# Sparse experts of a two-layer graph network: full-width weight loads in the up product and full-height ones in the down product

## The chip, the cores and the metric

The kernel is one program on one core of one Trainium2 chip. The metric is the device time of one execution in microseconds (us), from runs on the chip; lower is better. Everything is float32 in the part that is changed.

## The reference, cut to what matters

The model has two layers, each a graph attention, a linear attention and a mixture of experts, over 3,125 nodes with 256 features. The last step of the second layer is the one that is changed: each node goes to the one expert of 32 that its router scores highest, through 64 hidden features and back to 256:

```python
idx = jnp.argmax(xf @ router_w.T + router_b, axis=-1)         # 32 experts
h = relu(einsum('nd,ndh->nh', xf, W1[idx]) + b1[idx])         # 256 -> 64
out = relu(einsum('nh,nhd->nd', h, W2[idx]) + b2[idx])        # 64 -> 256
```

## The kernel before, in words

The program is a row of stages, each with its own block of engine programs; all engines meet between two stages. The stage here is `experts_l1` (L2651), between the router (`finish_route_l1`) and `combine_l1`. The router has sorted the nodes by expert into 56 tiles of 128 rows (`slots1` in device memory), each tile with one expert, whose number stands in `K.expert_at`. `combine_l1` gathers the results back to the nodes (L2816, 25 indirect transfers on POOL), adds the layer's input (L2823) and writes the output.

`experts_l1` handles tile j in slot q = j mod 4 of its buffers:

- SP loads the expert's weights `w[:, q, :]` (L2678): per partition 2 x 64 columns of the up matrix (two halves of 64 columns, one for each half of the 256 input features), then 256 columns of the down matrix. The down matrix has 64 weight rows, row 64 is its bias, and rows 65 to 127 are zeros that the host puts there.
- ACT loads the tile's rows (L2731), two tiles ahead in its own program. Both loads of a slot wait for the down product of the tile that used the slot four tiles before (`s_y`).
- PE turns the rows over (`turn_rows`, L2687, two transposes against the identity), multiplies by the up weights (`up`, L2695, two float32 products; each is recorded as two weight loads and two matmuls) and by the down weights (`down`, L2702, one product, likewise two and two). Its order is fixed: `turn_rows(j+1)`, `up(j)`, `down(j-1)`, again and again. `turn_rows` waits for both loads of its tile.
- DVE copies the turned rows out of PSUM (L2760) and takes the relu of the result (L2767); ACT takes the relu of the hidden features with the up bias (L2748) into `h_t[0:64]`. Row 64 of `h_t` is set to one at the stage's start (L2782), for the down bias.
- POOL stores the result (L2799), and waits at the end for all stores.

The stationary operand of `up` is the up weights: 128 rows by 64 columns, with 128 moving columns of turned features. The stationary operand of `down` is `h_t[0:65]`: 65 rows by 128 columns, with 256 moving columns of down weights.

Of the kernel before, what the change touches and what calls it, by code (L numbers as in the profile page):

```python
# [26 lines left out]
P = 128  # L27
N = 3125
D = 256
# [21 lines left out]
E1, F1 = 32, 64  # L51
# [2599 lines left out]
def experts_l1(prog, K, A):  # L2651

    with Stage(prog, "moe1") as st:
        Q, U2 = 4, 2
        sizes = {"rows": D, "w": 2 * F1 + D, "xs_t": 2 * P, "h_t": P, "y": D}
        at, tile = 0, {}
        for name, n in sizes.items():
            tile[name] = K.arena_a[:, at:at + Q * n].rearrange("p (q n) -> p q n", q=Q)
            at += Q * n
        rows, w, xs_t, h_t, y = tile.values()  # L2660
        w1, w2 = w[:, :, 0:2 * F1], w[:, :, 2 * F1:]
        b1 = st.sbuf("b1", [F1, E1])
        ps_t, ps_h, ps_y = (st.psum(n, [P, U2, 512]) for n in ("ps_t", "ps_h", "ps_y"))
        s_in = [st.sem(f"in{q}") for q in range(Q)]
        s_out = [st.sem_sw(f"out{q}") for q in range(Q)]
        s_b, s_one, s_t, s_xt, s_h, s_ht, s_y, s_yb = (st.sem(n) for n in ("b", "one", "t", "xt", "h", "ht", "y", "yb"))
        turns = T1 // Q
        block = st.block()

        @block.sync  # L2670
        def _(sp):
            sp.dma_start(b1[:, :], A["f1_b1"]).then_inc(s_b, 16)
            with sp.Fori(0, turns) as i:
                for q in range(Q):
                    j = i * Q + q
                    expert = sp.value_load(K.expert_at[0:1, bass.ds(j, 1)], min_val=0, max_val=E1 - 1)
                    sp.wait_ge(s_y, j + 1)
                    sp.dma_start(w[:, q, :], A["f1_w"][expert]).then_inc(s_in[q], 16)  # L2678

        @block.tensor  # L2680
        def _(pe):
            def turn_rows(i, q):
                j = i * Q + q
                pe.wait_ge(s_in[q], 32 * (i + 1))
                pe.wait_ge(s_xt, j + 1)
                for k in range(2):
                    ins = pe.transpose(ps_t[:, q % U2, k * P:(k + 1) * P], rows[:, q, k * P:(k + 1) * P], K.ident[:, :])  # L2687
                ins.then_inc(s_t, 1)

            def up(i, q):  # L2690
                j = i * Q + q
                pe.wait_ge(s_xt, j + 1 + U2)
                pe.wait_ge(s_ht, j + 1)
                for k in range(2):
                    ins = pe.matmul(ps_h[0:F1, q % U2, 0:P], lhsT=w1[:, q, k * F1:(k + 1) * F1], rhs=xs_t[:, q, k * P:(k + 1) * P], start=(k == 0), stop=(k == 1))  # L2695
                ins.then_inc(s_h, 1)

            def down(i, q):
                j = i * Q + q
                pe.wait_ge(s_ht, j + 1 + U2)  # L2700
                pe.wait_ge(s_yb, j + 1)
                pe.matmul(ps_y[:, q % U2, 0:D], lhsT=h_t[0:F1 + 1, q, :], rhs=w2[0:F1 + 1, q, :], start=True, stop=True).then_inc(s_y, 1)  # L2702

            def turn(i, head=False, tail=False):
                for q in range(Q):
                    if q + 1 < Q:
                        turn_rows(i, q + 1)
                    elif not tail:
                        turn_rows(i + 1, 0)
                    up(i, q)  # L2710
                    if q:
                        down(i, q - 1)
                    elif not head:
                        down(i - 1, Q - 1)

            pe.sem_inc(s_h, Q)
            pe.sem_inc(s_y, Q)
            pe.wait_ge(s_one, 1)
            turn_rows(0, 0)
            turn(0, head=True)  # L2720
            with pe.Fori(0, turns - 2) as i:
                turn(i + 1)
            turn(turns - 1, tail=True)
            down(turns - 1, Q - 1)

        @block.scalar
        def _(act):
            def load(i, q):
                j = i * Q + q
                act.wait_ge(s_y, j + 1)  # L2730
                act.dma_start(rows[:, q, :], K.slots1[bass.ds(j * P, P), :]).then_inc(s_in[q], 16)  # L2731

            act.sem_inc(s_ht, U2)
            load(0, 0)
            load(0, 1)
            act.wait_ge(s_b, 16)

            def turn(i, tail=False):
                for q in range(Q):
                    j = i * Q + q  # L2740
                    if q + 2 < Q:
                        load(i, q + 2)
                    elif not tail:
                        load(i + 1, q + 2 - Q)
                    expert = act.value_load(K.expert_at[0:1, bass.ds(j, 1)], min_val=0, max_val=E1 - 1)
                    act.wait_ge(s_h, j + 1 + Q)
                    act.wait_ge(s_y, j + 1)
                    act.activation(h_t[0:F1, q, :], ps_h[0:F1, q % U2, 0:P], ACT.Relu, bias=b1[:, bass.ds(expert, 1)]).then_inc(s_ht, 1)  # L2748

            with act.Fori(0, turns - 1) as i:  # L2750
                turn(i)
            turn(turns - 1, tail=True)

        @block.vector
        def _(dve):
            def turned(i, q):
                j = i * Q + q
                dve.wait_ge(s_t, j + 1)
                dve.wait_ge(s_h, j + 1)
                dve.tensor_copy(xs_t[:, q, :], ps_t[:, q % U2, 0:2 * P]).then_inc(s_xt, 1)  # L2760

            def result(i, q, stored=True):
                j = i * Q + q
                dve.wait_ge(s_y, j + 1 + Q)
                if stored:
                    dve.wait_ge(s_out[q], 16 * i)
                dve.tensor_scalar(y[:, q, :], ps_y[:, q % U2, 0:D], 0.0, None, ALU.max).then_inc(s_yb, 1)  # L2767

            def turn(i, tail=False):
                for q in range(Q):  # L2770
                    if q + 1 < Q:
                        turned(i, q + 1)
                    elif not tail:
                        turned(i + 1, 0)
                    if isinstance(i, int) and i * Q + q == 0:
                        continue
                    back = (i, q - 1) if q else (i - 1, Q - 1)
                    result(*back, stored=not (isinstance(i, int) and back[0] == 0))

            dve.sem_inc(s_xt, U2)  # L2780
            dve.sem_inc(s_yb, U2)
            dve.memset(h_t[F1:F1 + 1, :, :], 1.0).then_inc(s_one, 1)  # L2782
            turned(0, 0)
            turn(0)
            turn(1)
            with dve.Fori(0, turns - 3) as i:
                turn(i + 2)
            turn(turns - 1, tail=True)
            result(turns - 1, Q - 1)

        @block.gpsimd
        def _(pool):
            st.clear_stale(pool)
            with pool.Fori(0, turns) as i:
                for q in range(Q):
                    j = i * Q + q
                    pool.wait_ge(s_yb, j + 1 + U2)
                    pool.nop(nofuse=True)
                    pool.dma_start(K.y_slots1[bass.ds(j * P, P), :], y[:, q, :]).then_inc(s_out[q], 16)  # L2799
            for q in range(Q):  # L2800
                pool.wait_ge(s_out[q], 16 * turns)
# [33 lines left out]
def stages(prog, K, A, out):  # L2835

    order_edges(prog, K, A)
    items_project_l0(prog, K, A)
    linear_attention_l0(prog, K, A)
    edge_scores_l0(prog, K, A)  # L2840
    segment_softmax(prog, K, "soft0", H0, C0, A=A)
    aggregate_l0(prog, K)
    finish_route_l0(prog, K, A)
    experts_l0(prog, K, A)
    join_project_l1(prog, K, A)
    linear_attention_l1(prog, K, A)
    for H, C, RW, table, kept, acc in ((H1, C1, H1 * (DH1 + 1), K.table1, K.kept1, K.acc1),
                                       (1, C2, D + 1, K.table2, K.kept2, K.acc2)):
        keep = K.al[:, WSP * H:WSP * (2 * H + 1)].rearrange("p (s h) -> p s h", h=H + 1)
        edge_scores_l1(prog, K, f"score_h{H}", H, C, RW, table, kept, A)  # L2850
        segment_softmax(prog, K, f"soft_h{H}", H, C, keep, RW, table, kept)
        aggregate(prog, K, f"sum_h{H}", H, RW, table, kept, acc, keep)
        if H == H1:
            middle_l1(prog, K, A)
    finish_route_l1(prog, K, A)
    experts_l1(prog, K, A)
    combine_l1(prog, K, out)
# [119 lines left out]
```

## Time and profile before

| | us |
|---|---|
| median of 3 runs (lowest, highest) | 3234.79 (3234.34 to 3239.66) |
| span of the profiled execution | 3241.8 |
| mean granted TensorE clock over the span | 0.801 |
| stage `experts_l1`, first turned tile to last down product | 3019.6 to 3190.0 |

The profiled execution's span is 7.0 us (0.2%) above the median of the runs; no other time is recorded for it. Its clock column gives the share of the full TensorE clock that was granted: 1.00 is 2.4 GHz, 0.50 is 1.2 GHz. PE is the matmul half of TensorE and PEld the weight loads. A DMA row ending in q is an issue, which isn't counted as busy time. The ends of matmuls are modelled, the starts are recorded.

### The profile page before, as it was taken

Reading aid. Unit: us, or ns where it says so; the run is one execution under the profiler, and the core shown is the slowest. Engines: PE = TensorE matmul, PEld = TensorE weight load, DVE = VectorE, ACT = ScalarE, POOL = GpSimd, SP = SyncE. Lnnn points to the kernel's source line nnn. Section 1 sums busy time; section 2 is a strip of 40 time slices with the busy share of each in tenths; the row PEclk is TensorE's granted clock in tenths of the full one; section 3 lists DMA queues with packets and bytes.
Section 4 is the critical chain, followed back from the end, with each engine's and each line's share of the span. In section 5 each row is a group of like instructions: output and inputs, shape, how many; then the busy total and the mean of one; then the engine's idle time right before and its main releaser. Section 6 shows DMA issues by size and latency. Waiting matters only on the chain. (4 is left out here: it accounts for less than half of the span.)

```text
span 3241.8 us, 48906 instructions
## 1 busy us (share of the span) xinstructions
PE 2228.9 (69%) x10992; PEld 1503.4 (46%) x10993; DVE 2056.2 (63%) x3849; ACT 1246.0 (38%) x3616; POOL 1722.4 (53%) x1802
## 2 busy tenths in 40 slices
PE   3635777767997389948673899997661766654693
PEld 2322333335555356535562677776551444433341
DVE  7587777778788343452677788887682666665221
ACT  2223333326775221234001666665201666652010
POOL 1586777733554301132554777774466777751213
PEclk9867787778999599979766999998765899885555
DMA  4768888874885278825996788886896555530454
GB/s 140 205 181 231 260 263 262 261 235 138 218 219 161 96 254 278 263 90 197 364 396 196 243 274 269 273 276 166 240 291 175 148 147 149 146 107 23 132 152 132
DMA packets 456713, 668.49 MB, mean 206 GB/s; under 512 B 67154, under 2 KB 334092, under 8 KB 456001
## 3 DMA queue, kind: packets, MB, share of 16 engines
q1 hardware_dynamic: 334017, 357.96, 36.3%
q0 software_dynamic: 87248, 261.86, 27.3%
q10 hardware_dynamic: 35296, 46.90, 4.1%
q8 instruction: 64, 1.05, 0.1%
q14 instruction: 88, 0.72, 0.1%
HBM read 491.69 MB, written 176.23 MB: 206 GB/s over the span
## 5 line engine op out<-in xcount | busy, mean ns | idle before, releaser
L1533 POOL DMA_INDIRECT xn<-table,src_col x572 | 595.8, 1042 | 180.6 <-issue 148.9
L1574 PE MATMUL sum_h_ps<-xn,sum_h_hot 128*128 128x261 f32 (+1 forms) x1936 | 526.5, 415 | 192.0 <-DVE xn L1588 128.8
L1574 PEld LDWEIGHTS sum_h_ps<-xn,sum_h_hot 128*128 128x128 f32 x1936 | 369.7, 201 | 341.3 <-DVE xn L1588 251.6
L1092 POOL DMA_INDIRECT arena_a<-table,src_col x264 | 265.6, 1006 | 267.7 <-issue 184.7
L978 POOL DMA_INDIRECT arena_b<-table,src_col x336 | 318.7, 949 | 111.7 <-issue 108.6
L1588 DVE TENSOR_TENSOR xn<-xn,al 128x514 f32<-128x514 f32 (+1 forms) x352 | 243.4, 692 | 167.9 <-DMA xn<-table,src_col 164.0
L1597 DVE TENSOR_TENSOR arena_a<-arena_a,sum_h_ps 128x522 f32 (+1 forms) x440 | 246.1, 559 | 62.1 <-issue 38.2
L1707 PE MATMUL sum_ps<-xn,sum_hot 128*128 128x264 f32 x880 | 245.4, 406 | 31.4 <-DVE arena_a L1730 10.4
L1690 POOL TENSOR_TENSOR xn<-xn,al 128x264 f32<-128x264 f32 x220 | 158.8, 723 | 168.5 <-DMA xn<-edge_h 165.5
L1009 ACT ACTIVATE xn<-score_ps_en 128x512 f32<-128x512 f32 x220 | 131.4, 597 | 291.1 <-PE score_ps_en L995 287.4
L999 PE MATMUL score_ps_hd<-arena_a,score_hot 128*128 x1320 | 238.8, 330 | 0.0
L1707 PEld LDWEIGHTS sum_ps<-xn,sum_hot 128*128 128x128 f32 x880 | 151.9, 191 | 124.6 <-issue 88.1
L995 PE MATMUL score_ps_en<-enc_rows,score_attr 30*128 30x256 bf16 x440 | 101.2, 317 | 130.8 <-DVE xn L1037 85.7
L1040 DVE TENSOR_REDUCE al<-xn 128x528 f32 (+1 forms) x220 | 154.7, 703 | 32.8 <-DVE xn L1037 32.0
L999 PEld LDWEIGHTS score_ps_hd<-arena_a,score_hot 128*128 128x128 bf16 x1320 | 129.1, 112 | 91.4 <-issue 61.3
L756 POOL DMA_INDIRECT xn<-table,src_col x104 | 124.9, 1201 | 84.8 <-issue 84.8
L1574 PE MATMUL sum_h_ps<-arena_b,sum_h_hot 128*128 128x261 f32 x704 | 166.8, 383 | 0.9 <-DVE arena_b L1588 0.6
L1559 ACT ACTIVATE xn<-xn,al 128x129 f32<-128x129 f32 x528 | 167.2, 388 | 0.0
L1555 ACT ACTIVATE xn<-al 128x4 f32<-128x4 f32 (+1 forms) x352 | 71.2, 203 | 238.3 <-DMA xn<-table,src_col 237.4
L1037 DVE TENSOR_TENSOR xn<-xn,score_ps_hd 128x528 f32<-128x528 f32 x220 | 153.4, 697 | 14.2 <-PE score_ps_hd L999 13.2
L1540 ACT ACTIVATE sum_h_away<-iota_row,rel_col 128x128 f32<-128x128 f32 x440 | 149.2, 386 | 11.1 <-DVE sum_h_one L1600 11.1
L2053 POOL DMA_DIRECT2D y_slots<-al x32 | 28.4, 888 | 220.0 <-DVE al L2029 219.9
(516 smaller groups left out, 4628.7 us busy)
## 6 DMA issues: line engine op xcount, KB each, us to landing
xn<-edge_h SPq DMA_DIRECT2D x220, 264.0 KB, 3.2
edge_h<-arena_b SPq DMA_DIRECT2D x84, 528.0 KB
arena_b<-kept SPq DMA_DIRECT2D x66, 516.0 KB, 5.4
xn_t<-edge_rows SPq DMA_DIRECT2D x110, 256.0 KB, 4.6
score_h_hot<-hots SPq DMA_DIRECT2D x220, 128.0 KB, 11.7
kept<-arena_a ACTq DMA_DIRECT2D x40, 516.0 KB, 9.1
xn<-kept SPq DMA_DIRECT2D x66, 257.0 KB
arena_a<-in_f_w SPq DMA_DIRECT2D x16, 1024.0 KB, 8.7
```

The lines of the kernel that those rows point to most:

```text
L978: pool.indirect_dma_start(rows[:, q, k, :], None, K.table0[:, :], bass.IndirectOffsetOnAxis(ap=K.src_col[:, g * GS + k:g * GS + k + 1], ax ...
L999: ins = pe.matmul(ps_hd[:, m, s, 0:D + H], lhsT=hot[:, q, edges[s]], rhs=near[:, window, c, :], start=(c == 0), stop=(c == 2))
L1037: dve.tensor_tensor(prod[:, m, :].rearrange("p (s d) -> p s d", s=SUB), enc[:, m, :].rearrange("p (s d) -> p s d", s=SUB), ps_hd[:, m, :, ...
L1040: dve.tensor_reduce(al[:, bass.ds(w * SUB, SUB), :], prod[:, m, :].rearrange("p (s h r) -> p s h r", s=SUB, h=H), AX, ALU.add).then_inc(s_ ...
L1092: pool.indirect_dma_start(rows[:, q, s, :], None, table, bass.IndirectOffsetOnAxis(ap=K.src_col[:, w * SUB + s:w * SUB + s + 1], axis=0)). ...
L1533: pool.indirect_dma_start(rows[w][:, s, 0:RW], None, table, bass.IndirectOffsetOnAxis(ap=K.src_col[:, w * SUB + s:w * SUB + s + 1], axis=0 ...
L1559: ins = act.activation(cols, cols, ACT.Copy, scale=al[:, w * SUB + 1, h:h + 1])
L1574: ins = pe.matmul(ps[:, u, b, 0:part], lhsT=hot[:, w % QH, s, :], rhs=rows[w][:, s, b * part:(b + 1) * part], start=(s == 0), stop=(s == S ...
L1588: dve.tensor_tensor(view, view, al[:, bass.ds(w * SUB, HALF), :].rearrange("p s h -> p (s h)").unsqueeze(2).broadcast_to([P, HALF * H, RW ...
L1597: dve.tensor_tensor(out, out, ps[:, j % U2, :, 0:part], ALU.add).then_inc(s_acc, 1)
L1690: pool.tensor_tensor(view, view, al[:, bass.ds(w * SUB + 1, 1), :].rearrange("p s h -> p (s h)").unsqueeze(2).broadcast_to([P, H, R]), ALU ...
L1707: ins = pe.matmul(ps[:, u, 0:ROW0], lhsT=hot[:, q, s, :], rhs=rows[:, q, s, :], start=(s == 0), stop=(s == SUB - 1))
```

## The change

`up` loads 128 columns in place of 64. The first of its two products takes columns 0 to 127 of the slot (both halves of the up matrix), the second columns 64 to 191 (the second half and 64 columns of the down matrix). It writes 128 partitions of PSUM, of which ACT reads the first 64 as before. `down` uses all 128 rows of `h_t` and of the down weights, whose rows 65 to 127 are zeros; so that those rows of `h_t` hold numbers, they are set to zero at the start of the stage, ahead of row 64.

```diff
-        w1, w2 = w[:, :, 0:2 * F1], w[:, :, 2 * F1:]
+        w2 = w[:, :, 2 * F1:]
...
-                    ins = pe.matmul(ps_h[0:F1, q % U2, 0:P], lhsT=w1[:, q, k * F1:(k + 1) * F1], rhs=xs_t[:, q, k * P:(k + 1) * P], start=(k == 0), stop=(k == 1))
+                    ins = pe.matmul(ps_h[:, q % U2, 0:P], lhsT=w[:, q, k * F1:k * F1 + P], rhs=xs_t[:, q, k * P:(k + 1) * P], start=(k == 0), stop=(k == 1))
...
-                pe.matmul(ps_y[:, q % U2, 0:D], lhsT=h_t[0:F1 + 1, q, :], rhs=w2[0:F1 + 1, q, :], start=True, stop=True).then_inc(s_y, 1)
+                pe.matmul(ps_y[:, q % U2, 0:D], lhsT=h_t[:, q, :], rhs=w2[:, q, :], start=True, stop=True).then_inc(s_y, 1)
...
+            dve.memset(h_t[F1:, :, :], 0.0).then_inc(s_zero, 1)
+            dve.wait_ge(s_zero, 1)
             dve.memset(h_t[F1:F1 + 1, :, :], 1.0).then_inc(s_one, 1)
```

## Rows read from the trace of the kernel before

**Rows 1.** The page: the granted clock in 40 slices of the span, in tenths.

```profile
PEclk9867787778999599979766999998765899885555
```

**Rows 2.** The chain that ended last, by line.

```profile
by line: POOL xn L2816 0.7%; issue 0.2%; DMA xn<-y_slots,slot_to 0.1%; DVE xn L2823 0.0%; POOLq L121 0.0%; PEldq L121 0.0%
```

**Rows 3.** Stretches: length, each engine's busy us (instructions), granted clock, DMA share, GB/s.

```profile
280.00:700.00 420.00, 312.83 (x1734) 151.39 (x1731) 330.95 (x557) 139.50 (x301) 310.08 (x327) 0.79 0.88 259
1140.00:1380.00 240.00, 220.35 (x773) 140.32 (x774) 95.47 (x139) 49.86 (x72) 26.80 (x29) 0.98 0.81 263
2500.00:2880.00 380.00, 260.85 (x840) 164.62 (x840) 232.52 (x419) 263.12 (x850) 289.81 (x297) 0.90 0.55 148
2915.00:2955.00 40.00, 31.59 (x148) 28.94 (x146) 27.80 (x96) 20.53 (x52) 0.00 (x0) 0.50 0.00 0
3020.00:3190.00 170.00, 158.42 (x448) 84.30 (x446) 46.87 (x111) 20.28 (x56) 29.20 (x54) 0.50 0.48 146
```

**Rows 4.** One such stretch of the first layer's edge scores.

```profile
425.00:435.00 10.00, 9.44 (x39) 4.28 (x40) 8.58 (x14) 3.22 (x7) 7.56 (x9) 0.50 0.82 256
```

**Rows 5.** Timeline of PE inside it.

```profile
427.53 0.60 PE L995 MATMUL score_ps_en<-enc_rows,score_attr 30*128 30x256 bf16 x2
428.06 1.50 PE L999 MATMUL score_ps_hd<-arena_a,score_hot 128*128 x6
```

**Rows 6.** Groups of the stage by form: rows*columns of the weights, shape, count, mean ns.

```profile
L2695 PEld LDWEIGHTS moe_ps_h<-arena_a 128*64 128x64 f32 x224 | 40.1, 218 | 18.8 <-issue 18.8
...
L2687 PEld LDWEIGHTS moe_ps_t<-ident,arena_a 128*128 128x128 f32 x112 | 16.2, 204 | 102.1 <-issue 75.5 <-DMA arena_a<-slots 23.2 <-DMA arena_a<-in_f_w 3.3
```

**Rows 7.** Timeline of the stage: start us, length us, what.

```profile
3024.41 1.22 PE L2702 MATMUL moe_ps_y<-arena_a 65*128 65x256 f32 x2
...
3105.20 0.68 PE L2687 MATMUL moe_ps_t<-ident,arena_a 128*128 128x128 f32 x2
...
3105.49 0.36 ACTq L2731 DMA_DIRECT2D arena_a<-slots  x1
3105.81 1.12 PE L2695 MATMUL moe_ps_h<-arena_a 128*64 128x128 f32 x4
...
3106.86 1.22 PE L2702 MATMUL moe_ps_y<-arena_a 65*128 65x256 f32 x2
...
3108.26 0.37 ACTq L2731 DMA_DIRECT2D arena_a<-slots  x1
...
3108.36 0.69 PE L2687 MATMUL moe_ps_t<-ident,arena_a 128*128 128x128 f32 x2 [0.28 <-DMA arena_a<-slots]
...
3111.35 0.69 PE L2687 MATMUL moe_ps_t<-ident,arena_a 128*128 128x128 f32 x2
...
3187.89 2.08 PE L2702 MATMUL moe_ps_y<-arena_a 65*128 65x256 f32 x4
```

**Rows 8.** DMA issues of the stage: count, KB each, median us to landing.

```profile
arena_a<-in_f_w SPq DMA_DIRECT2D x54, 192.0 KB, 2.7
...
arena_a<-slots ACTq DMA_DIRECT2D x53, 128.0 KB, 2.9
```

**Rows 9.** Timeline: runs of like float32 matmuls in other stages, at either clock.

```profile
179.79 6.38 PE L774 MATMUL mix_ps_c<-arena_a 128*128 128x128 f32 x52
204.70 4.64 PE L774 MATMUL mix_ps_c<-arena_a 128*128 128x128 f32 x20 [18.54 <-DVE arena_a L850]
...
1165.06 7.17 PE L2002 MATMUL moe_ps_y<-arena_a,arena_b 128*128 128x256 f32 x32 [0.62 <-DVE al L2029]
```

**Rows 10.** The stretch that holds the second of those runs.

```profile
200.00:220.00 20.00, 4.64 (x20) 4.34 (x20) 18.36 (x16) 2.67 (x2) 16.34 (x13) 0.50 0.60 172
```

**Rows 11.** Groups of weight loads over the whole span: the longest mean.

```profile
L1835 PEld LDWEIGHTS route_ps_l<-route_gw,xn_t 128*128 128x128 f32 x100 | 24.1, 333 | 1.0 <-ACT xn_t L1861 1.0
```

**Rows 12.** Timeline of the stage's start.

```profile
3015.61 0.48 DVE L2782 MEMSET arena_a<- 1x512 f32 x1 [33.32 <-PEq L2716]
...
3019.63 0.66 PE L2687 MATMUL moe_ps_t<-ident,arena_a 128*128 128x128 f32 x2 [53.74 <-DMA arena_a<-in_f_w]
```

More of the change, by code:

```diff
@@ L2665, in experts_l1 @@
         s_out = [st.sem_sw(f"out{q}") for q in range(Q)]
-        s_b, s_one, s_t, s_xt, s_h, s_ht, s_y, s_yb = (st.sem(n) for n in ("b", "one", "t", "xt", "h", "ht", "y", "yb"))
+        s_b, s_zero, s_one, s_t, s_xt, s_h, s_ht, s_y, s_yb = (st.sem(n) for n in ("b", "zero", "one", "t", "xt", "h", "ht", "y", "yb"))
         turns = T1 // Q
```

## The prediction

> **What bounds the kernel now.** I read the page first. Its clock line [rows 1] ends in four slices at 5: the last 320 us run at half of TensorE's clock, and `experts_l1` lies in them. The chain that ended last [rows 2] names only the closing gathers of `combine_l1`. These begin when all engines have met behind `experts_l1`, so a microsecond taken from that stage is one taken from the kernel, as long as the stores behind the last tile keep their length.
>
> Then the stretches [rows 3]. In the stage PE is busy 158.42 of 170 us (93%), with a granted clock of 0.50 (1.2 GHz) from end to end. No long stretch with full weights looks so: 1140 to 1380, the first layer's experts, has PE at 92% and 0.98; 2500 to 2880 has PE at only 69% and still 0.90. What differs is the size of the weights. In the stage they are 128 rows by 64 columns and 65 rows by 128 columns, beside transposes of 128 by 128 [rows 6, 7]; in the experts of the first layer they are nearly all 128 by 128. The stretch from 280 to 700 lies between: its loop has two matmuls over 30 rows for each six over 128 [rows 5], PE is busy 74%, and the clock 0.79. For 425 to 435 us PE was busy 94% there and the clock stayed at 0.50 [rows 4]. So in this trace a TensorE that is busy by the record, with part of its rows unused, is held at 1.2 GHz, and one with full weights isn't. The trace can't say whether rows or columns do it; the change fills both.
>
> That PE is 93% busy doesn't make it the only bound. The timeline [rows 7] shows the loop of one tile as turn, up, down. The down products start at 3024.41 and, for the last two, from 3187.89 on; 54 steps lie between, so a tile takes 163.48 / 54 = 3.03 us. PE's own work of one turn is shorter: turn to up 3105.20 to 3105.81 (0.61), up to down 1.05, down's 1.22 with 0.1 of it overlapped by what follows, about 2.8. The rest is waiting for the row load: a turn starts at 3108.36 on "DMA arena_a<-slots". The load of tile j+3 is issued when `down(j-1)` has ended, and is wanted two turns on. So two tiles take (start of a turn to the issue) + (issue to the start of the turn that wants it): 3105.20 to 3108.26 is 3.06; 3105.49 to 3108.36 is 2.87 and 3108.26 to 3111.35 is 3.09, mean 2.98. Together 6.04, half of it 3.02, which is the measured 3.03. The landings agree: 2.9 and 2.7 us in the median for rows and weights [rows 8]. What PE gains comes out at half its size per tile, since it shortens only the first part of that two-tile loop.
>
> **The change part by part.** *Arithmetic and DMA.* No instruction, wait or transfer is added in the loop; the host's zeros were loaded already. The counts stay as they are.
>
> *Streaming.* The moving columns stay at 128 and 256, so at an equal clock the matmuls take what they took.
>
> *Weight loads of up, 64 to 128 columns.* This is the part that could cost. In L774, also float32 with 128 moving columns but 128 weight columns, 20 matmuls took 4.64 us at 0.50 [rows 9, 10]: (4.64 - 0.42 for the last one's length) / 19 = 0.222 us each. The loads lie hidden beside the matmuls. Up's four take 1.05 us to the start of down with the change to another wait in it, so they run at that step already. In this stage the transposes' 128-column loads take 204 ns against 218 for up's 64 columns [rows 6]. I take 0. Bound above: the longest mean of a 128x128 float32 load in the trace, 333 ns [rows 11], less 218 is 0.115 each, 0.46 per up group, if fully exposed.
>
> *Rule against the change.* The rows show 204 ns for 128 columns and 218 for 64. The Trainium skill, "TensorE: Matmul & The Clock Gate", section "LDWEIGHTS (loading the stationary operand)", says that a load takes its number of columns divided by 1.2 ns whatever its rows; by that up's loads would grow by an estimated 53 ns a pass, and the down loads not at all. The trace disagrees for the durations as recorded. By this rule, with all exposed, the loop would be slower by an estimated 0.1 us a tile.
>
> *Down over 128 rows.* Rows are parallel; 0. Nothing below 0 is excluded for its loads, but they have no measured share of the loop.
>
> *Memset.* One more of 64 partitions by 512, beside the one of 1 by 512 that took 0.48 us, and a wait [rows 12]. Call it 0.5 to 1.0. It ends by 3017.1 where PE's first turn waits for the weights' DMA until 3019.63. Hidden, with 2.5 us to spare; uncovered it would cost at most 1 us.
>
> *The clock.* With full weights I expect the 0.50 to end. The worth of 1.00 from pairs of rows [rows 9]: L774 at 1.00 takes (6.38 - 0.28) / 51 = 0.120 us per 128 moving columns, against 0.222; L2002 at 1.00 takes (7.17 - 0.38) / 31 = 0.219 for 256. So each 128 columns saves 0.102. From the start of a turn to the issue lie two of 128 (turn), four of 128 (up), two of 256 (down): ten units, 1.02 us; the last matmul's tail shortens too (0.42 to 0.28, the two subtracted lengths, of which the streaming step explains 0.10), so 1.02 to 1.15, say 1.1. Two tiles then take 6.04 - 1.1 = 4.94, a tile 2.47 in place of 3.02: 0.55 us less. PE's own turn is then about 2.8 - 1.1 = 1.7, so the DMA loop still binds, now alone. Over 54 steps at full clock for all: 30 us.
>
> *How much of the stage gets it.* At 1.00 PE would be busy some 1.7 to 1.75 of 2.47 us, 70%; the stretch from 2500 to 2880, full weights at 69% busy, has 0.90. Then it isn't sure how soon the half-clock loop with its waits wakes the clock; 280 to 700 comes to 0.79. And here, a faster PE only waits longer for its row loads in each turn, after which a fall is likelier. Between 0.50 and 1.00 I take a mean of 0.75: half of 30 us, 15 us. DMA isn't in the way: its share is 0.48 [rows 3] and would rise to 0.48 x 3.02 / 2.75 = 0.53, and POOL's stores are a third of the bytes.
>
> **The sum.** 0 + 0 + 0 (memset hidden) - 15 = -15 us. Against the profiled execution: 3241.8 - 15 = 3226.8. That execution is 7.0 us above the median of the runs and no row says why; the same difference from the median gives 3234.8 - 15 = 3220.
>
> **The rivals.** *A, my forecast:* the clock goes up and down in the stage, mean 0.6 to 0.93; 54 x 0.55 x (0.2 to 0.86) = 6 to 26 us: 3209 to 3229.
>
> *B, full clock nearly throughout.* For it: 0.98 to 1.00 in the other stages with full weights. Against it: those don't wait 0.7 us in every tile for a DMA. 26 to 32 us off: 3203 to 3209.
>
> *C, the change doesn't do what it can: the clock stays at 0.50.* For it: the router's short matmuls from 2915 to 2955 have full weights too, PE 79% busy, and 0.50 [rows 3]; and the stage waits on its loads already. Then 0, and 3234 to 3236. The Trainium skill, same page, "Part 1: The HAM clock gate", says that the clock gate is opened by how busy PE has been and says nothing of the weights' size; by that rule 93% busy would have had full clock before, and filling the weights would change nothing. The trace disagrees on the first half with its 0.50.
>
> *D, the other side: up's weight loads become the step.* Place: between the four matmuls of `up`. They decide once a 128-column load takes longer than the 0.222 us of the matmul beside it. Price: up to 0.46 a group, in the two-tile loop 0.23 a tile, 54 x 0.23 = 12 us, 3247, with the clock unchanged. Against it: L774's 20 matmuls at 0.222 with such loads [rows 9].
>
> **How the numbers follow.** A 0.58, B 0.13, C 0.24, D 0.03, and 0.02 for anything else that is slower. 0.2% of the time, 6.5 us, is about what a measurement of this kernel can tell from no change. A gives faster but for its lower edge (0.02 of it within), B faster: 0.69. C with A's edge gives the same: 0.26. D and the rest give slower: 0.05. The likeliest is A's middle, 3220. The range reaches from B, 3203, to C's end, 3236, and leaves out D.
>
> **What would show each step.** The granted clock over 3020 to 3190 in the new profile: A says 0.6 to 0.93, with whole stretches of ten us at 1.00, C 0.50. Step of `down` to `down`: 2.4 to 2.5 us where the clock is 1.00, still 3.0 where it is 0.50 (D: 3.2). The recorded loads of up: near 200 ns at 0.50. Turns that wait on "DMA arena_a<-slots" or "in_f_w" in nearly every tile, and issue to landing still 2.7 to 3.0. The first turn still released by a DMA, not by L2782's memset. All before the stage unchanged. The prediction fails on its size if the clock's mean is far from 0.75, and in its mechanism if the clock rises and the step of a tile doesn't fall by half of PE's saving, or if landings grow as the loads come closer together.

## The result and the profile after

The changed kernel takes 3197.29 us in the median (3192.84 to 3198.91, 4 runs), the kernel before 3234.57 (3228.68 to 3239.66, 4 runs). The ratio is 0.9877, with a 95% interval of 0.9861 to 0.9893: 37 us or 1.2% faster. That is below the low end of the range, 3203, and more than twice the 15 us of the forecast.

The whole stage after, as one stretch (length, busy us and instructions of PE, PEld, DVE, ACT and POOL, granted clock, DMA share, GB/s):

```profile
3013.00:3145.70 132.70, 84.22 (x448) 60.85 (x448) 46.86 (x111) 20.28 (x56) 29.22 (x54) 0.91 0.62 186
```

The same stretch of before, from the first turn to the last down product, has 170.4 us at 0.50; [rows 3] show nearly the same. So 37.7 us went in the stage, which is the gain of the medians. The profiled spans differ by 44.5 (3241.8 to 3197.3), and the first turn starts at 3013.07 in place of 3019.63: that 6.6 us lies ahead of the changed code. In the kernels run below, whose code is the same up to there, the first turn starts anywhere from 3012.7 to 3028.4, so it is scatter.

The clock isn't at 1.00 throughout. Ten-microsecond stretches of the stage after:

```profile
3010.00:3020.00 10.00, 5.17 (x20) 4.08 (x21) 1.88 (x6) 0.72 (x2) 0.59 (x1) 0.50 0.51 142
3020.00:3030.00 10.00, 7.03 (x35) 4.91 (x34) 3.34 (x9) 1.45 (x4) 2.11 (x4) 0.80 0.62 184
...
3040.00:3050.00 10.00, 6.21 (x39) 4.20 (x37) 3.99 (x10) 1.81 (x5) 2.18 (x5) 1.00 0.66 205
...
3090.00:3100.00 10.00, 6.35 (x31) 4.81 (x31) 3.08 (x8) 1.45 (x4) 2.06 (x5) 0.83 0.60 183
```

The groups by form, to be held against [rows 6]:

```profile
L2695 PEld LDWEIGHTS moe_ps_h<-arena_a 128*128 128x128 f32 x224 | 34.6, 221 | 0.2
...
L2687 PE MATMUL moe_ps_t<-ident,arena_a 128*128 128x128 f32 x112 | 26.9, 325 | 102.1 <-DMA arena_a<-in_f_w 56.4 <-DMA arena_a<-slots 45.7
...
L2702 PEld LDWEIGHTS moe_ps_y<-arena_a 128*128 128x128 f32 x112 | 19.5, 218 | 0.6 <-ACT arena_a L2748 0.6
```

The number behind the last bar is the loader's idle time, and it is the surprise. Before, the weight loader stood idle for 18.8 us ahead of up's loads, put down to "issue" [rows 6]; now it is 0.2. Ahead of down's loads 18.4 us before (first line below) have become 0.6. The turns wait 45.7 us for the row loads: the two-tile loop binds. The kernel before, a whole-stage group and two lines of its timeline:

```profile
L2702 PEld LDWEIGHTS moe_ps_y<-arena_a 65*128 65x128 f32 x112 | 28.3, 313 | 18.4 <-issue 18.2
```

```profile
3105.81 0.72 PEld L2695 LDWEIGHTS moe_ps_h<-arena_a 128*64 128x64 f32 x4 [0.33 <-issue]
...
3106.86 0.50 PEld L2702 LDWEIGHTS moe_ps_y<-arena_a 65*128 65x128 f32 x2 [0.33 <-issue]
```

The timeline after, first at 0.50 and then at 1.00, to be held against [rows 7]:

```profile
3019.17 0.69 PE L2687 MATMUL moe_ps_t<-ident,arena_a 128*128 128x128 f32 x2 [1.02 <-DMA arena_a<-slots]
...
3021.45 0.69 PE L2687 MATMUL moe_ps_t<-ident,arena_a 128*128 128x128 f32 x2
...
3021.72 0.97 PEld L2695 LDWEIGHTS moe_ps_h<-arena_a 128*128 128x128 f32 x4
3021.74 0.38 ACTq L2731 DMA_DIRECT2D arena_a<-slots  x1
3021.93 1.06 PE L2695 MATMUL moe_ps_h<-arena_a 128*128 128x128 f32 x4
...
3022.78 1.06 PE L2702 MATMUL moe_ps_y<-arena_a 128*128 128x256 f32 x2
...
3112.75 0.37 ACTq L2731 DMA_DIRECT2D arena_a<-slots  x1
3113.26 0.44 PE L2687 MATMUL moe_ps_t<-ident,arena_a 128*128 128x128 f32 x2 [0.69 <-DMA arena_a<-slots]
...
3113.53 0.61 PE L2695 MATMUL moe_ps_h<-arena_a 128*128 128x128 f32 x4
...
3113.98 0.60 PE L2702 MATMUL moe_ps_y<-arena_a 128*128 128x256 f32 x2
...
3114.75 0.38 ACTq L2731 DMA_DIRECT2D arena_a<-slots  x1
3115.61 0.20 PEld L2687 LDWEIGHTS moe_ps_t<-ident,arena_a 128*128 128x128 f32 x2 [1.44 <-DMA arena_a<-slots]
...
3117.89 0.43 PE L2687 MATMUL moe_ps_t<-ident,arena_a 128*128 128x128 f32 x2 [0.96 <-DMA arena_a<-slots]
```

At 0.50 up to down is 3022.78 - 3021.93 = 0.85 us, where it was 1.05 at the same clock [rows 7], and start of a turn to the issue of a load is 3019.17 to 3021.74 = 2.57 in place of 3.06. Up's first load begins at 3021.72, 0.21 ahead of its matmul at 3021.93; before, load and matmul both began at 3105.81. So the change took time away at an equal clock too, which the prediction didn't have. At 1.00 start of a turn to issue is 3113.26 to 3114.75 = 1.49, and issue to the turn that wants it 2.86 and 3.14 (3112.75 to 3115.61, 3114.75 to 3117.89): (1.49 + 3.0) / 2 = 2.25 us a tile. Over the stage the down products start 2.35 us apart, counted as in the prediction: (3144.22 - 3017.09) / 54. The rest is the part at 0.50.

### The profile page after: what moved, and what is told of

The parts are those of the page before. It is cut to its first block and busy times, and to the rows that moved or that the text cites. A ratio compares the mean times of both kernels' runs of the same rounds, so it can differ in the third digit from the quotient of the medians.

```text
span 3197.3 us, 48907 instructions
## 1 busy us (share of the span) xinstructions
PE 2147.4 (67%) x10992; PEld 1473.6 (46%) x10993; DVE 2060.7 (64%) x3850; ACT 1246.2 (39%) x3616; POOL 1712.0 (54%) x1802
## 3 DMA queue, kind: packets, MB, share of 16 engines
q8 instruction: 64, 1.05, 0.1%
## 5 line engine op out<-in xcount | busy, mean ns | idle before, releaser
L1533 POOL DMA_INDIRECT xn<-table,src_col x572 | 587.4, 1027 | 180.6 <-issue 150.1
L756 POOL DMA_INDIRECT xn<-table,src_col x104 | 124.3, 1195 | 85.4 <-issue 84.7
```

The source lines that it names most:

```text
L1533: pool.indirect_dma_start(rows[w][:, s, 0:RW], None, table, bass.IndirectOffsetOnAxis(ap=K.src_col[:, w * SUB + s:w * SUB + s + 1], axis=0 ...
```

## The experiments

Two theories stood: all of the gain is the clock; or PE lost time at up's and down's odd shapes, at either clock, and the clock is only a part. Each experiment was timed against the kernel before.

### 1. Up alone

```diff
# against before
-                    ins = pe.matmul(ps_h[0:F1, q % U2, 0:P], lhsT=w1[:, q, k * F1:(k + 1) * F1], rhs=xs_t[:, q, k * P:(k + 1) * P], start=(k == 0), stop=(k == 1))
+                    ins = pe.matmul(ps_h[:, q % U2, 0:P], lhsT=w[:, q, k * F1:k * F1 + P], rhs=xs_t[:, q, k * P:(k + 1) * P], start=(k == 0), stop=(k == 1))
```

> Up loads 128 columns; down keeps its 65 rows, no extra memset. Clock theory (all of the gain is the granted clock): if columns open it, about 0.9 in the stage and some 30 us off; if rows or the whole area do, 0.50 and 0 us. Shape theory (PE loses time wherever neighbouring weights differ in shape, at either clock): turn to up falls from 0.61 to 0.43 us and up's first step from 0.268 to 0.213, up to down stays near 0.35 after the last matmul of up, and the two-tile loop gives back 0.1 us a tile, 5 us in all, at 0.50.

Measured: 3219.44 us, ratio 0.9952 (0.9935 to 0.9969), 15.5 us off. The stage, and its groups by form:

```profile
3012.60:3164.30 151.70, 126.55 (x448) 89.90 (x448) 47.15 (x112) 20.28 (x56) 29.20 (x54) 0.55 0.53 163
```

```profile
L2695 PEld LDWEIGHTS moe_ps_h<-arena_a 128*128 128x128 f32 x224 | 52.4, 321 | 0.1
```

The clock hardly moves (0.55), and the loader's idle time is gone with up alone. The timeline has start of a turn to issue 2.57 us and up to down 0.86:

```profile
3100.82 0.69 PE L2687 MATMUL moe_ps_t<-ident,arena_a 128*128 128x128 f32 x2 [0.51 <-DMA arena_a<-slots]
...
3101.30 1.06 PE L2695 MATMUL moe_ps_h<-arena_a 128*128 128x128 f32 x4
...
3102.16 1.06 PE L2702 MATMUL moe_ps_y<-arena_a 65*128 65x256 f32 x2
...
3103.39 0.37 ACTq L2731 DMA_DIRECT2D arena_a<-slots  x1
```

The gain is three times the 5 us that the shape theory asked for. The late start inside down goes too (its two matmuls take 1.06 us in place of 1.22), though down still has 65 rows. So it was never down's rows that cost time there; it was that up's narrow weights stood before it. The loop gives 0.49 / 2 = 0.25 us a tile, 54 x 0.25 = 13 us. The rest, 2 to 3 us, is what a clock of 0.55 is worth: full clock for a tenth of the stage, 0.1 x 0.55 x 54 = 3 us by the prediction's price.

### 2. Down alone

```diff
# against before, with the memset of the change
-                pe.matmul(ps_y[:, q % U2, 0:D], lhsT=h_t[0:F1 + 1, q, :], rhs=w2[0:F1 + 1, q, :], start=True, stop=True).then_inc(s_y, 1)
+                pe.matmul(ps_y[:, q % U2, 0:D], lhsT=h_t[:, q, :], rhs=w2[:, q, :], start=True, stop=True).then_inc(s_y, 1)
```

> Down uses 128 rows, with the memset; up keeps its 64 columns. Clock theory by rows: the clock is near 0.9 and 25 to 30 us are off; by area or columns: 0.50 and 0 us. Shape theory: the step between down's two matmuls falls from 0.588 to 0.427 us, turn to up stays 0.61 (at 0.50), 0.08 us a tile less, 4 us in all without the clock.

Measured: 3211.69 us, ratio 0.9928 (0.9904 to 0.9951), 23 us off.

```profile
3014.60:3158.50 143.90, 106.86 (x448) 59.64 (x448) 46.76 (x111) 20.30 (x56) 29.35 (x54) 0.87 0.56 172
```

```profile
L2695 PEld LDWEIGHTS moe_ps_h<-arena_a 128*64 128x64 f32 x224 | 27.3, 157 | 12.2 <-issue 12.2
L2702 PEld LDWEIGHTS moe_ps_y<-arena_a 128*128 128x128 f32 x112 | 18.9, 212 | 11.5 <-issue 11.2 <-ACT arena_a L2748 0.3
```

Filling the rows brings the clock to 0.87; the loader's idle time stays. At 1.00 up to down is 3106.73 - 3106.15 = 0.58 us here, where the changed kernel has 0.45, and down's pair takes 0.70 against 0.60:

```profile
3101.32 1.22 PE L2702 MATMUL moe_ps_y<-arena_a 128*128 128x256 f32 x2
...
3106.15 0.65 PE L2695 MATMUL moe_ps_h<-arena_a 128*64 128x128 f32 x4
3106.73 0.70 PE L2702 MATMUL moe_ps_y<-arena_a 128*128 128x256 f32 x2
```

The forecast of the shape theory for this run, a shorter step inside down, missed: at 0.50 down's pair still takes 1.22 us (at 3101.32), as before the change. The drops of the ratio of the two halves, 0.0048 and 0.0072, add up to 0.0120; both together gave 0.0123.

The medians over the stage, from one matmul's start to the next one's, in ns, say the same with all tiles counted:

| | before, 0.50 | up alone, 0.50 | down alone, 0.50 | down alone, 1.00 | both, 1.00 |
|---|---|---|---|---|---|
| last transpose to up | 351 | 213 | 351 | 202 | 109 |
| up's first to its second | 268 | 214 | 269 | 160 | 112 |
| up's last to down | 351 | 213 | 350 | 202 | 112 |
| down's first to its second | 588 | 427 | 589 | 320 | 218 |

At 0.50 the four steps lose 0.49 us together where up has 64 columns, with 65 rows in down or with 128.

### 3. The kernel before, with each transpose issued twice

```diff
# against before
-                for k in range(2):
+                for k in (0, 1, 0, 1):
                     ins = pe.transpose(ps_t[:, q % U2, k * P:(k + 1) * P], rows[:, q, k * P:(k + 1) * P], K.ident[:, :])
```

> The shapes of the kernel before, but each transpose is issued twice (the same result twice into the same place), so PE streams 0.43 us more per tile at 1.2 GHz and its waits close. Clock theory: more use of the full array may open the clock without any change of up or down; then the stage has 0.8 or more and the kernel is 20 us faster although it does more work. If the clock stays at 0.50, the loop is (3.06 + 0.43 + 2.98) / 2 = 3.24 us a tile, 12 us slower than before. Shape theory: if the clock does rise, the steps from turn to up and up to down stay over 0.2 us at 1.00, where the changed kernel has 0.11.

Measured: 3249.82 us, ratio 1.0041 (1.0025 to 1.0058), 15 us slower.

```profile
3015.40:3198.30 182.90, 179.76 (x560) 108.96 (x560) 47.18 (x112) 20.32 (x56) 29.35 (x54) 0.50 0.44 136
```

PE is 98% busy and stays at 0.50. The down products start (3196.14 - 3020.97) / 54 = 3.24 us apart, which is what the loop gave in advance. More work on the full array in the transposes didn't open the clock. Transposes may count for less than products, so this run alone doesn't settle what a busy TensorE gets; experiment 5 makes PE as busy with no transpose added.

### 4 and 5. Eight slots, and row loads four tiles ahead

```diff
# the same for the changed kernel (4) and for the kernel before (5)
-        Q, U2 = 4, 2
+        Q, U2, AHEAD = 8, 2, 4
...
-            load(0, 0)
-            load(0, 1)
+            for q in range(AHEAD):
+                load(0, q)
...
-                    if q + 2 < Q:
-                        load(i, q + 2)
+                    if q + AHEAD < Q:
+                        load(i, q + AHEAD)
                     elif not tail:
-                        load(i + 1, q + 2 - Q)
+                        load(i + 1, q + AHEAD - Q)
```

> The changed kernel with eight slots in place of four and the row loads issued four tiles ahead in place of two, so that no load waits for a fresh down product. If the two-tile loop through the row load sets the step of 2.38 us, it goes, and the step falls to what the DMA engines need, 0.62 of 2.38 = 1.5 us a tile, over PE's own turn of about 1.2 at full clock: 1.5 to 1.7, the granted clock 0.95 or more in the stage, the kernel 35 to 45 us faster than the changed one. If the loop was not the bound, no change.

> The kernel before with the same eight slots and loads four tiles ahead. Only PE's own turn is left: 2.78 us a tile (0.61 + 1.05 + 1.12) in place of 3.03, PE busy over 99%, and the clock still 0.50, because neither rows nor columns are filled: 14 us faster than before. If the clock followed PE's recorded busy time, it would open here and the step would fall below 2 us.

Measured: (4) 3154.99 us, ratio 0.9746 (0.9729 to 0.9762); (5) 3219.76 us, ratio 0.9942 (0.9926 to 0.9959). The stage of (4), and then of (5):

```profile
3017.80:3105.20 87.40, 78.44 (x448) 57.87 (x448) 44.33 (x111) 20.30 (x56) 29.19 (x54) 0.97 0.87 280
```

```profile
3019.80:3168.00 148.20, 147.28 (x448) 93.43 (x448) 46.36 (x111) 20.32 (x56) 29.22 (x54) 0.50 0.55 166
```

In (5) the loop through the loads is gone and PE is 99% busy, still at 0.50: 65 rows in down and 64 columns in up, no waits, no full clock. Its own turn shows in the timeline:

```profile
3101.80 0.63 PE L2687 MATMUL moe_ps_t<-ident,arena_a 128*128 128x128 f32 x2
3102.37 1.12 PE L2695 MATMUL moe_ps_h<-arena_a 128*64 128x128 f32 x4
3103.41 1.22 PE L2702 MATMUL moe_ps_y<-arena_a 65*128 65x256 f32 x2
3104.43 0.63 PE L2687 MATMUL moe_ps_t<-ident,arena_a 128*128 128x128 f32 x2
```

3104.43 - 3101.80 = 2.63 us, less than the 2.78 expected: a turn whose rows are there long before starts 1.02 us after down, not 1.12, and up starts 0.57 us after it, not 0.61. The kernel gained 17 us for the 14 expected.

In (4) the down products start (3103.79 - 3021.75) / 54 = 1.52 us apart. That is near the DMA time per tile of the changed kernel (0.62 x 2.35 = 1.46), but the DMA share is 0.87, PE is 90% busy, and the loader waits for ACT ahead of down's loads:

```profile
L2702 PEld LDWEIGHTS moe_ps_y<-arena_a 128*128 128x128 f32 x112 | 17.0, 191 | 10.5 <-ACT arena_a L2748 9.1 <-issue 0.4 <-DVE arena_a L2767 0.3
```

Which of the three sets the 1.52 stays open. It is the fastest kernel here, 42 us below the changed one. The number of slots and the lead of the loads were changed together; the waits of the turns for the row loads, 45.7 us in the changed kernel, are 3.7 us here, which is the loop that bound that one.

### 6 and 8. Up with 127 and with 96 columns

```diff
# against after; 96 in place of 127 in the second
-                    ins = pe.matmul(ps_h[:, q % U2, 0:P], lhsT=w[:, q, k * F1:k * F1 + P], rhs=xs_t[:, q, k * P:(k + 1) * P], start=(k == 0), stop=(k == 1))
+                    ins = pe.matmul(ps_h[0:127, q % U2, 0:P], lhsT=w[:, q, k * F1:k * F1 + 127], rhs=xs_t[:, q, k * P:(k + 1) * P], start=(k == 0), stop=(k == 1))
```

> The changed kernel, but up loads 127 columns in place of 128. If the lost time comes from a change in the number of weight columns between neighbours, or from any number short of 128, the steps into and out of up are long again (0.35 us at 1.2 GHz, 0.20 at 2.4 GHz in place of 0.21 and 0.11) and the kernel takes what the version with only down changed took, 3212. If only a half-filled array costs it, the time is the changed kernel's, 3197.

> The changed kernel, but up loads 96 columns. 127 columns kept the short steps, 64 had the long ones. If any width that leaves a quarter of the array's columns unused costs the time, turn to up is 0.35 us after the last transpose at 1.2 GHz (0.20 at 2.4) and down's first step 0.59 (0.32), and the kernel takes about what 64 columns took with a full down product, 3212. If only half the array or less does, the steps are 0.21 (0.11) and 0.43 (0.22) and it takes 3197. The clock should be near 0.9 in either case, all rows being used.

Measured: 127 columns 3200.65 us, ratio 0.9883 (0.9867 to 0.9900); 96 columns 3198.66, ratio 0.9873 (0.9844 to 0.9901). Both are the changed kernel's, within their intervals. Up's loads with 127 columns, then with 96:

```profile
L2695 PEld LDWEIGHTS moe_ps_h<-arena_a 128*127 128x127 f32 x224 | 34.4, 220 | 0.1
```

```profile
L2695 PEld LDWEIGHTS moe_ps_h<-arena_a 128*96 128x96 f32 x224 | 30.7, 181 | 0.3
```

The loader's idle time is gone at either width, and up to down is 0.44 us at 1.00 in both. So the lost time needs neither a full array to go away nor neighbours of equal width: 64 columns of 128 cost, 96 don't. What lies between wasn't tried, and why a load of 64 columns waits no run shows. The clock with 96 columns is 0.93:

```profile
3020.00:3150.00 130.00, 79.56 (x446) 56.74 (x446) 46.49 (x110) 20.20 (x56) 28.66 (x53) 0.93 0.63 192
```

### 7. Down with 96 rows

```diff
# against after
-                pe.matmul(ps_y[:, q % U2, 0:D], lhsT=h_t[:, q, :], rhs=w2[:, q, :], start=True, stop=True).then_inc(s_y, 1)
+                pe.matmul(ps_y[:, q % U2, 0:D], lhsT=h_t[0:96, q, :], rhs=w2[0:96, q, :], start=True, stop=True).then_inc(s_y, 1)
```

> The changed kernel, but down uses 96 rows of h_t and of its weights (65 hold numbers, 31 are zeros). No lost time at the change of shape, since all weights have 128 columns: steps as in the changed kernel. If unused rows hold the clock back in proportion, it lies between 0.55 (65 rows) and 0.91 (128 rows), near 0.7, and the kernel near 3208. If it needs all rows, it stays near 0.55 and 3219.

Measured: 3211.81 us, ratio 0.9923 (0.9907 to 0.9940).

```profile
3014.00:3152.40 138.40, 96.11 (x448) 70.00 (x448) 47.09 (x112) 20.28 (x56) 29.21 (x54) 0.80 0.59 179
```

With 65, 96 and 128 rows in down, and up full, the kernel took 3219, 3212 and 3197 us in the median. The stage's clock was 0.55, 0.80 and 0.91 in the profiled executions. With 96 rows that was the fastest of the four, 3205.35 us; the others took 3211 to 3213 us with a lower mean clock over the whole program (0.808 to 0.812, against 0.822), so 0.80 goes with 3205 and not with 3212. So more rows give more full clock by degrees; in each trace the clock switches between its two levels within the stage.

## Why the prediction was wrong, point by point

**The bound.** Right. The two-tile loop through the row load gave 3.02 for a measured 3.03, and halves whatever PE saves. The deeper buffers confirm it: without the loop the same PE work runs at 1.52 us a tile. Only PE's own turn was read 0.15 too long, 2.78 for 2.63 (experiment 5), which changed nothing in the sum.

**The clock.** Right in its mechanism and in its worth: full weights ended the 0.50, and from experiment 1 at 0.50 to the changed kernel at 1.00 the start of a turn to the issue falls from 2.57 to 1.49 us, 1.08 for a forecast 1.1. The prediction left open whether rows or columns do it. It is the rows in the main: filling down's rows alone gave 0.87, filling up's columns alone 0.55. The Trainium skill, "TensorE: Matmul & The Clock Gate", "Part 1: The HAM clock gate", has the clock set by how busy PE has been. By the busy time of the record the runs disagree, with PE 98 and 99% busy at 0.50 in experiments 3 and 5. Full rows aren't enough by themselves either. The router's stretch, which the prediction gave as the ground for rival C, stays at 0.50 in the changed kernel too, with PE 69% busy; its products have 128 rows and stream only 32 columns each. Why it isn't at full clock no run tested. The stretch after, and one of its products in the trace of before:

```profile
2915.00:2955.00 40.00, 27.77 (x126) 25.00 (x125) 26.88 (x78) 16.57 (x42) 0.00 (x0) 0.50 0.00 0
```

```profile
2930.35 0.90 PE L2565 MATMUL route_ps_l<-route_rw,xn_t 128*128 128x32 f32 x4
```

**The step that failed: "Weight loads of up, 64 to 128 columns. ... I take 0."** Its bounds were 0 and a loss; nothing excluded a gain, and the prediction named none. In fact up's 64-column weights cost time: around them the loader stood idle (18.8 us ahead of up's loads alone, [rows 6]), and PE started later with up, with the second matmul of up, with down and with the second of down. Experiment 1 measures it at nearly the same clock: 3.06 to 2.57 us from the start of a turn to the issue, 0.25 us a tile. At 1.00 the start of a turn to the issue was forecast at 3.06 - 1.1 = 1.96 us and is 1.49, about 0.23 a tile. That is 54 x 0.23 = 12 us of the 22 that were missed. The signs stood in the rows: at 0.50 L774's matmuls with 128 columns followed each other every 0.222 us [rows 9], so up's four should have reached down in 4 x 0.222 = 0.89, and took 1.05. The prediction put that 0.16 down to "the change to another wait in it", but in the changed kernel the same wait stands there and up to down takes 0.85. The loader's idle time put down to "issue" [rows 6] was the other sign, and the prediction passed over it.

**How much of the stage gets it.** The second term that was off. A mean of 0.75 was taken, 0.91 measured, inside rival A's 0.6 to 0.93. At 0.91 the share at full clock is 0.82, and 0.55 x 0.82 x 54 = 24 us, 9 more than forecast. 24 + 12 = 36 us is the stage's 37.7 but for 2 us. Rival B's price, 32 us at most, was too small for the same reason.

**Memset, DMA.** Right. The two memsets took 0.49 us each, and a DMA released the first turn. Landings stayed at 3.0 and 2.6 us in the median.

**The other side.** D did not come. The recorded mean of up's loads did grow in experiment 1, 218 to 321 ns, against the "near 200 ns" that the prediction wanted to see; but they lie beside the matmul ahead of them, and the steps became shorter. The Trainium skill, same page, "LDWEIGHTS (loading the stationary operand)", has a load take longer the more columns it has. The direction agrees here, but the longer load didn't make the loop slower.

## What to carry to other kernels

Before costing a wider weight at nothing or at a loss, compare the start-to-start times of the matmuls with the plain streaming step of a full-width run at the same clock: what a narrow weight takes beyond that step is what padding it can give back. Where TensorE is busy at the lower clock, look at the rows of its weights; zero rows that are loaded anyway cost nothing to use here, and they counted for the clock though they add only zeros. And where a load waits for the compute of an earlier tile, ask how many tiles that loop spans: here it halved PE's gain, and deeper buffers were worth more (42 us) than the change itself (37 us).

## What the runs showed of the hardware that was not expected

- Float32 weights of 64 columns (128 rows) between weights of 128 columns: the matmuls into, inside and behind them start later, 0.49 us for each turn of eight matmuls at 1.2 GHz and 0.33 us at 2.4 GHz (the table in experiment 2). With 96, 127 or 128 columns it is gone. Weights of 65 rows (128 columns) don't cause it.
- In this stage the granted clock follows the rows in use and hardly the columns: down with 65, 96, 128 rows gave 0.55, 0.80, 0.91 (up full); up with 64, 96, 127, 128 columns gave 0.87, 0.93, 0.91, 0.91 (down full), each in one profiled execution. PE's busy share of the record was 99% at 0.50 in one kernel and 63% at 0.91 in the changed one. Rows that hold only zeros count as in use: rows 65 to 127 of down do (0.50 to 0.87 in experiment 2).
